# Bulk loads on another engine's DMA queue, the first keys split on another engine, and the first stacks loaded in halves, in a two-attention kernel on one core

## The chip, the cores and the metric

The kernel runs on one core of one Trainium2 chip. The metric is the time on the device of one execution, in microseconds (us), lower is better.

## The reference

The input x is 16 x 256 x 128 in float32 (16 batches, T = 256 rows, D = 128). Four blocks follow each other, each adding to x:

```
x = x + attention_a(layernorm(x))     # softmax, q and k rotated by position (rope), 16 heads of 8
x = x + ffn(layernorm(x))             # silu(x Wg) * (x Wu), then Wd; integer weights / 127, hidden 384
x = x + attention_b(layernorm(x))     # causal, sparsemax instead of softmax, 16 heads of 8
x = x + ffn(layernorm(x))
```

## The kernel before

**Items and steps.** The work is cut into 32 items: item n below 16 is the softmax attention and the feed-forward of batch n ("soft"), item n from 16 on the sparsemax attention and feed-forward of batch n - 16. All engines run one list of steps, `for step in range(FIRST_STEP, LAST_STEP)`, each doing what is its own in a step. An item has 16 heads and starts 16 steps behind the one before it. `AT`, `PLAIN` and `SECOND` say at which step (16 n + offset) each piece of item n is due; `SECOND` has the offsets of item 1. Engines meet at semaphores alone, and each engine executes its own list in order. Steps below 0 are the lead-in: they make the queries and keys of items 0 and 1. From step 0 on, step 16 n + h forms head h's scores of item n (`pass1`, line 1452, two products), whose row maxima VectorE takes (`reduce_head`, line 1093). From step 30 on, `pass2` forms the scores again, transposed and with the maxima subtracted (line 1476), ScalarE takes the exponential (`probs`, line 1288), and `pv` (line 1498) multiplies by the values.

**Queries and keys of an item.** TensorE transposes the normalised x (line 1354), ScalarE copies it (`take_xT`, line 1233), TensorE projects q, k and v (lines 1368, 1378). VectorE adds the rotation's two terms (`rope_cos`, `rope_sin`, lines 1080, 1086). GpSimd adds them and splits the float32 result into three bf16 parts (`split`, lines 928 to 938: add, cast, subtract, cast, subtract). SyncE stores the parts in device memory (`store_q`, lines 778 and 779, 192 and 128 KB; `store_k`, line 784, 192 KB) and loads them back, rearranged, as stacks (`load_q` and `load_k`, lines 792 and 809, three transfers of 192 KB each). `pass1` of an item waits at head 0 until all six transfers are there. Four sets of stacks (`STACKS`) take turns. SyncE issues every transfer of the kernel, in one order; `load_shift` (line 813) brings the row maxima into the stacks and sits behind `load_q` of a later item.

**Once only.** Weights, constants and the later x are loaded by SyncE at steps given in `ONCE` and `X_REST`: wb 449 KB, two pieces of constants of 256 and 384 KB, wf 576 KB; x of items 3 and 4 (256 KB), 5 to 7 (384 KB), 8 to 11 and 12 to 15 (512 KB each). `load_mask_rows` (line 801) makes eight transfers of 384 KB, one every 16 steps from step 57 on. VectorE casts the masks and the weights at steps 24 and 40.

**Spare products.** `spare` (line 1506) is a product of the identity with itself whose result nobody reads. 34 of them are issued at step -16, 60 at step -10, and four in each of the steps 0 to 28 that have no projection or transposition (22 such steps).

## Time and profile before

| | |
|---|---|
| median of 3 runs | 628.57 us |
| the three runs | 627.22, 628.57, 633.52 us |
| profiled execution: span from first to last instruction | 625.7 us |
| median less that span | 2.9 us |
| TensorE busy | 596.2 us (95%) |
| VectorE, ScalarE, GpSimd busy | 487.5, 427.1, 390.2 us |

The profile records one execution. Its own time is not listed apart from its span, so the table sets the span beside the median: the 2.9 us are what lies around the span and what this execution was faster or slower than the median.

### The profile page before, as it was taken

To read this page: it belongs to the slowest core of one execution; us is meant where nothing else is said; L and a number is where in the kernel's file an instruction comes from. 1 tells how busy PE (TensorE), PEld (TensorE's weight loads), DVE (VectorE), ACT (ScalarE), POOL (GpSimd) and SP (SyncE) were. 2 spreads that over 40 slices of the span, in tenths; PEclk is the share of its full clock that TensorE was granted. 3 is DMA by queue.
4 is the path that set the end of the run, shared out by engine and by line. 5 is a ranking of instruction groups with operands and counts; after the bars stand their busy time and mean duration, and the time that the engine had idled before them with its cause. 6 is when DMAs were issued, how large, how long until landed. Compare 5 with 4: busy or idle time off the path is not lost.

```text
span 625.7 us, 19158 instructions
## 1 busy us (share of the span) xinstructions
PE 596.2 (95%) x6716; PEld 465.1 (74%) x6716; DVE 487.5 (78%) x1421; ACT 427.1 (68%) x1057; POOL 390.2 (62%) x824
## 2 busy tenths in 40 slices
PE   5897999999999999999999999999999999999985
PEld 4775556777677777676778888788888888888664
DVE  2297788888888888888788887787888888888332
ACT  2013677777877777788878777676777777777762
POOL 5754456676776666767766766577666666653332
PEclk9997999999999999999999999999999999999996
DMA  3597467766566645554454533433544444440000
GB/s 98 131 260 170 118 155 178 174 150 153 152 143 157 144 121 119 149 143 134 123 141 124 133 95 97 119 104 84 123 111 121 111 116 106 114 120 20 13 10 21
DMA packets 73760, 75.91 MB, mean 121 GB/s; under 512 B 10236, under 2 KB 68156, under 8 KB 69052
## 3 DMA queue, kind: packets, MB, share of 16 engines
q1 hardware_dynamic: 73660, 74.64, 47.3%
q8 instruction: 55, 0.90, 0.6%
q14 instruction: 45, 0.37, 0.2%
HBM read 46.86 MB, written 23.33 MB: 112 GB/s over the span
## 4 chain that ended last, share of the span: by engine, by line
PE 73%; DMA 6%; DVE 5%; issue 5%; POOL 4%; ACT 3%; SPq 2%; POOLq 0%; ACTq 0%; DVEq 0%
PE banks L1498 15%; PE banks L1476 8%; PE banks L1452 8%; PE banks L1429 7%; PE banks L1368 5%; PE banks L1420 4%; PE banks L1421 3%; PE banks L1455 3%; PE banks L1461 2%; PE banks L1400 2%; PE banks L1485 2%; PE banks L1479 2%; DMA q_image<-qk_parts 2%; PE banks L1457 2%; PE banks L1459 2%
## 5 line engine op out<-in xcount | busy, mean ns | idle before, releaser
L1288 ACT ACTIVATE probs_t<-banks 128x512 f32<-128x512 f32 (+1 forms) x512 | 270.4, 550 | 82.5 <-PE banks L1476 53.8
L1093 DVE TENSOR_REDUCE neg_shift<-banks 128x2 f32<-128x512 f32 x256 | 166.3, 681 | 42.5 <-PE banks L1452 41.2
L1498 PE MATMUL banks<-probs_t,v_ext 128*32 128x256 f32 (+1 forms) x2048 | 117.8, 359 | 0.0
L1452 PE MATMUL banks<-k_stack,q_stack 72*128 72x256 bf16 x512 | 100.5, 278 | 6.7 <-DVE neg_shift L1093 2.5
L1099 DVE MAX8 top<-banks 128x8 f32<-128x256 f32 x256 | 106.1, 415 | 0.0
L1476 PE MATMUL banks<-q_stack,k_stack 75*128 75x256 bf16 x512 | 100.1, 277 | 1.0 <-DMA q_stack<-neg_shift_rows 0.9
L984 POOL TENSOR_TENSOR hidden<-up_tanh,gate_half 128x256 f32<-128x256 f32 x96 | 69.9, 731 | 48.1 <-DVE up_tanh L1139 42.2
L1098 DVE MAX8 top<-banks 128x8 f32<-128x128 f32 x256 | 74.5, 291 | 31.6 <-PE banks L1461 29.2
L1498 PEld LDWEIGHTS banks<-probs_t,v_ext 128*32 128x32 f32 x2048 | 55.5, 109 | 40.1 <-issue 13.3
L1452 PEld LDWEIGHTS banks<-k_stack,q_stack 72*128 72x128 bf16 x512 | 41.3, 98 | 45.8 <-DVE neg_shift L1093 32.8
L1420 PE MATMUL banks<-f_xT_high,w_gate_up 128*128 128x256 f32 x192 | 58.8, 328 | 0.9 <-DVE f_xT_low L1131 0.9
L1479 PE MATMUL banks<-q_stack,k_stack 123*128 123x128 bf16 x256 | 57.0, 223 | 2.8 <-ACT probs_t L1288 2.2
L1461 PE MATMUL banks<-mask_b,ident_b 128*128 128x160 bf16 x256 | 59.6, 233 | 0.0
L1485 PE MATMUL banks<-maskT_b,ident_b 128*128 128x160 bf16 x256 | 59.6, 233 | 0.0
L1455 PE MATMUL banks<-k_stack,q_stack 123*128 123x128 bf16 x256 | 56.6, 221 | 2.6 <-DVE top L1099 2.5
L1481 PE MATMUL banks<-q_stack,k_stack 75*128 75x128 bf16 x256 | 56.3, 220 | 0.0
L1457 PE MATMUL banks<-k_stack,q_stack 72*128 72x128 bf16 x256 | 56.2, 220 | 0.0
L1459 PE MATMUL banks<-k_stack,q_stack 123*128 123x128 bf16 x256 | 56.1, 219 | 0.0
L1483 PE MATMUL banks<-q_stack,k_stack 123*128 123x128 bf16 x256 | 56.1, 219 | 0.0
L916 POOL TENSOR_TENSOR f_rstd<-f_var_eps,neghalf 128x2 f32<-128x2 f32 x32 | 23.0, 720 | 50.3 <-DVE f_var_eps L1071 50.2
L928 POOL TENSOR_TENSOR qk<-rope_cos_terms,rope_sin_terms 128x256 f32<-128x256 f32 x32 | 23.2, 725 | 49.9 <-DVE rope_sin_terms L1086 49.8
L1476 PEld LDWEIGHTS banks<-q_stack,k_stack 75*128 75x128 bf16 x512 | 46.6, 99 | 10.2 <-issue 1.2
(108 smaller groups left out, 1389.4 us busy)
## 6 DMA issues: line engine op xcount, KB each, us to landing
q_stack<-q_image SPq DMA_DIRECT2D x96, 192.0 KB
k_stack<-k_image SPq DMA_DIRECT2D x96, 192.0 KB
q_image<-qk_parts SPq DMA_DIRECT2D x32, 192.0 KB, 2.3
k_image<-qk_parts SPq DMA_DIRECT2D x32, 192.0 KB, 2.1
q_image<-qk_parts SPq DMA_DIRECT2D x32, 128.0 KB, 2.2
o_image<-out_t SPq DMA_DIRECT2D x32, 128.0 KB, 1.9
out_compact<-o_image SPq DMA_DIRECT2D x32, 64.0 KB
rdenominators<-r_image SPq DMA_DIRECT2D x16, 128.0 KB, 2.3
```

The costliest lines, as they stand in the source:

```text
L984: pool.tensor_tensor(m.hid[:, c, :], m.t1[:, k, :], m.g05[:, k, :], ALU.mult).then_inc(hid_ready, 1)
L1093: dve.tensor_reduce(m.nm[:, n % STACKS, h, :], scores.rearrange("p (q k) -> p q k", q=TT), AX.X, ALU.max, negate=True).then_inc(reduced, 1)
L1098: dve.max(m.z8[:, n % 2, h, 0, :], scores[:, 0:P])
L1099: dve.max(m.z8[:, n % 2, h, 1, :], scores[:, P:P + T]).then_inc(reduced, 1)
L1288: act.activation(m.pt[:, (n * Q + g) % GROUPS, i, 0:size], shifted_banks[:, j % 2, 0:size], ACT.Exp if is_soft(n) else ACT.Relu, scale=SCA ...
L1420: pe.matmul(out, w[:, c * P:(c + 1) * P], m.f_high[:, :], start=True, stop=False)
L1452: ins = pe.matmul(scores[:, qt * T:(qt + 1) * T], qs[0:STACK, h, qt * P:(qt + 1) * P], ks[0:STACK, h, :], start=True, stop=True)
L1455: pe.matmul(scores[:, 0:P], qs[0:MASKED, h, 0:P], ks[0:MASKED, h, 0:P], start=True, stop=True, skip_group_check=True)
L1461: ins = pe.matmul(blocks(scores, REST), m.ident_b[:, :], twice(m.mask_b, REST), start=False, stop=True, skip_group_check=True)
L1476: ins = pe.matmul(shifted[:, kt * T:(kt + 1) * T], ks[0:SHIFTED, j, kt * P:(kt + 1) * P], qs[0:SHIFTED, j, :], start=True, stop=True)
L1485: ins = pe.matmul(blocks(shifted, REST), m.ident_b[:, :], twice(m.maskT_b, REST), start=False, stop=True, skip_group_check=True)
L1498: ins = pe.matmul(out_bank[32 * i:32 * i + 32, at + skip:at + T], v_windows(v, kt)[:, Q * g + i, :], m.pt[:, (n * Q + g) % GROUPS, i, kt * ...
```

## The change

Five edits:

1. The bulk loads (x from item 3 on, wb, two pieces of constants, wf) and the eight `load_mask_rows` are issued by ScalarE instead of SyncE. wb, the constants, wf and x of items 3 and 4 are due at step -22, which is behind ScalarE's copy of item 0 at step -23. Items 5 to 7 of x are due at step 1 (before at 11).
2. `split_k` of item 0 moves from GpSimd to VectorE, where it stands right behind item 0's `rope_sin` for the keys and ahead of item 1's statistics.
3. Item 0's stacks are loaded in two halves of heads, 12 transfers of 96 KB in place of six of 192 KB. The order on SyncE is: queries heads 0 to 7, queries heads 8 to 15, keys heads 0 to 7, keys heads 8 to 15. `pass1` of item 0 waits for the first halves at head 0 and for the second halves at head 8.
4. The four loads of ones into the key stacks (line 860) move from step -7 to step -31, ahead of all stores.
5. Spare products: 12 instead of 60 at step -10, three instead of four in the steps from 0 on; the 34 at step -16 stay.

```
-ONCE = dict(set_v=-14, ones=-7, wb=6, masks=8, wf=12, sum_bias=20, fold_bias=22, cast_masks=24, cast_weights=40)
-X_REST = {1: (3, 5), 11: (5, 8), 27: (8, 12), 43: (12, 16)}
-SPARE = {-16: 34, -10: 60}
-SPARE_SCORES = 4
+ONCE = dict(set_v=-14, ones=-31, bulk=-22, sum_bias=20, fold_bias=22, cast_masks=24, cast_weights=40)
+X_REST = {-22: (3, 5), 1: (5, 8), 27: (8, 12), 43: (12, 16)}
+SPARE = {-16: 34, -10: 12}
+SPARE_SCORES = 3
...
             def store_q(n):
                 sp.wait_ge(q_split, n + 1)
                 wait(sp, q_loaded, q_loads(n) * SEM)
+                if n == 1:
+                    sp.wait_ge(first_q_loaded, PARTS * SEM)
...
             def load_q(n):
...
+                first = H // 2 if n == 0 else 0
+                for rep in range(PARTS if n == 0 else 0):
+                    rows = slice(rep * PARTS * HD, (rep + 1) * PARTS * HD)
+                    sp.dma_start(m.qs[r][rows, 0:first, :], q_rows[rep * HD:(rep + PARTS) * HD, 0:first])\
+                      .then_inc(first_q_loaded, SEM)
                 for rep in range(PARTS):
                     rows = slice(rep * PARTS * HD, (rep + 1) * PARTS * HD)
-                    sp.dma_start(m.qs[r][rows, :, :], q_rows[rep * HD:(rep + PARTS) * HD]).then_inc(q_loaded, SEM)
+                    sp.dma_start(m.qs[r][rows, first:H, :], q_rows[rep * HD:(rep + PARTS) * HD, first:H])\
+                      .then_inc(q_loaded, SEM)
...
-                if (n := due(step, "split_k")) is not None:
+                if (n := due(step, "split_k")) is not None and n > 0:
                     split(n, 1)
...
+            def split_first_k():
+                qk = m.qk[:, 1, :]
+                high, middle, low = (m.parts[:, s, 1, :] for s in range(PARTS))
+                wait_freed(dve, "k", 0)
+                dve.tensor_tensor(qk, m.tc[:, 1, :], m.ts[:, 1, :], ALU.add).then_inc(k_step, 1)
+                dve.wait_ge(k_step, 1)
+                dve.tensor_copy(high, qk).then_inc(k_step, 1)
+                dve.wait_ge(k_step, 2)
+                dve.tensor_tensor(qk, qk, high, ALU.subtract).then_inc(k_step, 1)
+                dve.wait_ge(k_step, 3)
+                dve.tensor_copy(middle, qk).then_inc(k_step, 1)
+                dve.wait_ge(k_step, 4)
+                dve.tensor_tensor(low, qk, middle, ALU.subtract).then_inc(k_split, 1)
...
                     rope_sin(n, 1, "k")
+                    if n == 0:
+                        split_first_k()
...
+            def load_weights():
+                act.dma_start(m.wb[:, :], io["wb"]).then_inc(wb_loaded, SEM)
+                act.dma_start(m.cc[:, CC["invk"]:], io["consts"][:, CC["invk"]:CC_COLS]).then_inc(masks_loaded, SEM)
+                act.dma_start(m.co[:, :], io["consts"][:, CC_COLS:]).then_inc(masks_loaded, SEM)
+                act.dma_start(m.wf_int[:, :], io["wf"]).then_inc(wf_loaded, SEM)
+
             for step in range(FIRST_STEP, LAST_STEP):
+                if step in X_REST:
+                    first, end = X_REST[step]
+                    act.dma_start(m.x[:, first * TT:end * TT, :], x_d[:, first * TT:end * TT, :])\
+                       .then_inc(x_rest_loaded[x_piece(first)], SEM)
+                if step == ONCE["bulk"]:
+                    load_weights()
+                n, j = divmod(step - 3 * H, H)
+                if 0 <= n < 2 * STACKS and j == 9:
+                    load_mask_rows(*divmod(n, 2))
                 if (n := due(step, "take_out")) is not None:
                     take_out(n)
...
-                if h == 0:
+                if n == 0 and h == 0:
+                    pe.wait_ge(first_q_loaded, PARTS * SEM)
+                    pe.wait_ge(first_k_loaded, PARTS * SEM)
+                if h == (H // 2 if n == 0 else 0):
                     pe.wait_ge(q_loaded, q_loads(n + 1) * SEM)
                     pe.wait_ge(k_loaded, (n + 1) * (3 * SEM))
```

`store_k` and `load_k` are changed as `store_q` and `load_q`; `load_mask_rows` is the same function with `act` in place of `sp`.

## Rows read from the trace of the kernel before

**Rows 1.** Stages: length; PE, PEld, DVE, ACT, POOL busy (count); clock; DMA share; GB/s.

```profile
28.18:54.13 25.95, 23.30 (x180) 17.67 (x181) 24.53 (x54) 3.20 (x9) 11.44 (x26) 1.00 0.76 206
54.13:78.00 23.87, 21.91 (x170) 13.57 (x170) 16.89 (x35) 13.92 (x29) 11.28 (x24) 0.79 0.62 143
...
102.00:160.00 58.00, 57.89 (x561) 41.86 (x562) 50.68 (x119) 44.34 (x103) 40.75 (x83) 1.00 0.65 154
```

**Rows 2.** The chain, 13 to 29 us: start, length, what.

```profile
13.69 0.68 POOL a_rstd L908
...
17.99 2.08 DMA k_image<-qk_parts
...
20.83 7.22 DMA k_stack<-k_image
```

**Rows 3.** Timeline of the lead-in: start, length, engine, line, operation, [idle before].

```profile
11.67 0.47 DVE L1086 SCALAR_TENSOR_TENSOR rope_sin_terms<-banks,wa,cc 128x256 f32<-128x256 f32 x1
...
14.14 0.49 SPq L779 DMA_DIRECT2D q_image<-qk_parts  x1
...
18.39 1.26 SPq L792 DMA_DIRECT2D q_stack<-q_image  x3
...
19.40 6.71 PE L1506 MATMUL banks<-ident_b 128*128 128x256 bf16 x60
...
28.18 0.38 PE L1452 MATMUL banks<-k_stack,q_stack 72*128 72x256 bf16 x2 [2.07 <-DMA k_stack<-k_image]
...
28.60 2.67 DVE L1093 TENSOR_REDUCE neg_shift<-banks 128x2 f32<-128x512 f32 x4 [8.50 <-PE banks L1452]
```

**Rows 4.** Two stretches: length, TensorE busy, clock, DMA share, GB/s.

```profile
8.00:14.00 6.00, 6.00 (x26) 1.00 0.00 0
...
33.00:48.00 15.00, 14.09 (x113) 1.00 0.90 260
```

**Rows 5.** The chain of waits, 0 to 110 us: two pieces.

```profile
41.70 6.54 DMA q_image<-qk_parts
...
102.73 1.00 PE banks L1498 x16
```

**Rows 6.** Timeline 49 to 68 us: SyncE's queue and TensorE.

```profile
49.42 0.73 SPq L813 DMA_DIRECT2D q_stack<-neg_shift_rows  x1
...
52.01 0.39 PE L1452 MATMUL banks<-k_stack,q_stack 72*128 72x256 bf16 x2 [0.76 <-DVE neg_shift L1093]
...
54.13 0.41 PE L1476 MATMUL banks<-q_stack,k_stack 75*128 75x256 bf16 x2 [0.86 <-DMA q_stack<-neg_shift_rows]
...
57.59 0.59 PE L1452 MATMUL banks<-k_stack,q_stack 72*128 72x256 bf16 x2 [1.35 <-issue]
...
60.10 0.63 PE L1452 MATMUL banks<-k_stack,q_stack 72*128 72x256 bf16 x2
...
60.96 0.63 PE L1452 MATMUL banks<-k_stack,q_stack 72*128 72x256 bf16 x2
...
61.95 1.94 PE L1498 MATMUL banks<-probs_t,v_ext 128*32 128x256 f32 x16
```

**Rows 7.** Where the clock falls and returns: length, TensorE busy, clock, DMA.

```profile
54.25:54.50 0.25, 0.25 (x3) 0.70 0.65 131
...
64.50:64.75 0.25, 0.25 (x4) 0.82 0.00 0
```

**Rows 8.** Lines of VectorE: duration ns min/median/max, first and last start.

```profile
L1110 DVE SCALAR_TENSOR_TENSOR top_sums<-top_sums,cc x16: 424/604/718, 322.5 to 580.3; 128x256 f32<-128x256 f32 x16
L1151 DVE CAST maskT_b<-x x1: 219/219/219, 48.2 to 48.2; 128x128 bf16<-128x128 f32 x1
```

**Rows 9.** Steady state near 207 us, and line 801 over the run.

```profile
206.72 0.37 ACT L1233 COPY a_xT<-banks 128x256 f32<-128x256 f32 x1
...
207.47 1.03 PE L1368 MATMUL banks<-a_xT,wa 128*128 128x256 f32 x4
...
L801 SPq DMA_DIRECT2D q_stack<-mask_rows x4: 672/678/688, 101.9 to 208.2; - x4
```

34 lines of the change are left out of this document (14 added, 20 removed).

## The prediction

> **What bounds the kernel now.** I read the table of stages first. Behind 102 us TensorE is the bound: 57.89 of 58.00 us busy, and the chain of waits holds hardly anything else there. Nothing in the change takes work from that part, so it can only start sooner, or be slowed. What can be won lies ahead of it. Up to 28.18 us no head is scored; between 28.18 and 54.13 VectorE is busy 24.53 of 25.95 us and TensorE 23.30, partly with spare products; from 54.13 to 78 TensorE's mean granted clock is 0.79 [rows 1].
>
> The chain then says what the lead-in waits for. GpSimd is done with item 0's queries at 13.69 us and, behind item 1's small statistics, with its keys just ahead of 17.99; the store of the keys takes 2.08 us; the last load of a key stack is issued at 20.83 and lands 7.22 us later [rows 2]. SyncE had issued the store of the queries by 14.63, but stood at the store of the keys, so that the query stacks went out only at 18.39 [rows 3]. TensorE fills the wait with 60 spare products until 26.11, idles 2.07 us and scores at 28.18 [rows 3].
>
> The third view is the stretch from 33 to 48 us, where the bulk loads are issued: the DMA engines are 0.90 busy at 260 GB/s, while from 8 to 14 us they move nothing [rows 4]. A store of item 2's queries in that stretch takes 6.54 us [rows 5], against 2.08 for the store of item 0's keys [rows 2]. SyncE waits for it before it issues the shift rows at 49.42 and item 2's keys behind them; TensorE idles 0.86 us for the first and 1.35 us ahead of 57.59, where item 2 begins, for the second by my reading (the profile says "issue") [rows 6]. The clock falls near 54.4 us and is back near 64.6 [rows 7], after TensorE had idled 0.76 us for VectorE ahead of 52.01 and 0.86 us ahead of 54.13 [rows 6].
>
> **The change part by part.** The sum is made against the profiled execution: 625.7 us of span, and the 2.9 us to the median that no edit touches.
>
> *Keys of item 0 on VectorE.* `rope_sin` ends at 12.14 [rows 3]. Five instructions follow. The nearest row to a 128x256 operation with two inputs in SBUF is line 1110, 0.42 to 0.72 us, median 0.60; the nearest cast is 128x128 at 0.22, so 128x256 costs 0.22 to 0.44 [rows 8]. Three at 0.50, two at 0.35 and five hand-overs of about 0.07 (the gaps of GpSimd's chain) give 2.55 us: the keys are split at 14.7 (bounds 14.0 and 15.5) and not at 17.97 or so, and their store follows that of the queries. What is queued behind it on VectorE is item 1's statistics, 1.0 us of work, now done near 15.7; GpSimd's `rstd_a`, which started at 13.69 [rows 2], then starts 2 us later, and ScalarE's normalisation and TensorE's transposition of item 1 likewise. Item 1 is scored 16 steps behind item 0, more than 10 us later than its queries are stored, which covers that. GpSimd, rid of 3.1 us of split, gives the time back to item 1.
>
> Here a rule speaks against the edit. The 0.42 to 0.72 us of line 1110 for one shape [rows 8] show that such an operation sometimes takes longer. The Trainium skill, "SBUF — State Buffer", on the engine side of SBUF, says that an operation of VectorE with two SBUF inputs and one of GpSimd that reads SBUF take a port pair in turn, as an exclusive lock, the loser fully blocked. By that rule the two splits, side by side from 12.2 to 13.7, would be served one after the other and both be done near 15.5, which delays the query store by about 1.3 us and takes 1.0 us off the sum below (622.1 instead of 621.1); the trace has no such pair to show it.
>
> *Loads of item 0.* SyncE no longer stands at the keys. The query store lands 2.1 us behind 14.14, at 16.2 to 16.6 us, and the loads start there instead of at 18.39. Before, 1152 KB took from 18.39 to 28.05: 2.1 us of latency and 7.56 us of transfer. Head 0 now needs all of the queries and half of the keys, 864 KB, because the second halves of the queries stand ahead of the first halves of the keys: 5.67 us. That gives 16.6 + 2.1 + 5.7 = 24.4, and 24.5 for the first score. Six more issues of about 0.4 us each fit beside this transfer, since the ninth is out at 20.4. I add 0.6 us for what of the bulk is still moving and for items 5 to 7 of x, whose 384 KB ScalarE now issues near 22 us. First score at 25.1 instead of 28.18: 3.1 us (bounds 1.0 and 4.2). The second halves land some 2 us later and are needed eight steps, over 5 us, later.
>
> *Ones ahead.* Four issues of SyncE move to where it has nothing else; they leave its queue behind the key loads. Worth nothing in themselves.
>
> *Bulk loads at step -22.* ScalarE issues five transfers, 1.92 MB, between 7.2 and about 10.5 us, with nothing due on it until item 1. At 260 GB/s [rows 4] they take 7.4 us, until about 16. The DMA engines were idle for most of this. The two stalls go [rows 6]: 0.86 + 1.35 = 2.2 us (bounds 0.9 and 2.2). What is late next at step 30 is VectorE, at step 32 the keys of item 2, which should land 2 to 4 us before TensorE asks for them, although 512 KB of x (items 8 to 11) leaves ScalarE at about the same moment.
>
> *Clock.* If the second idle gap before 54.4 goes, I expect the clock to stay. At the low level two heads of item 2 are 0.86 us apart [rows 6], at the high level VectorE's pace is 0.67 [rows 3]; eight steps give 1.5 us. The sixteen products of line 1498 take 1.94 us there [rows 6], 1.00 at the high level [rows 5]. Together 2.4, of which I take 2.0, since VectorE and ScalarE are late next (bounds 0 and 3).
>
> *Fewer spares in the steps.* 22 steps lose 0.11 us of TensorE each, 2.4 us. But VectorE needs 0.63 to 0.67 per step, so most is not on the path; 0.8 us (bounds 0 and 2).
>
> *Mask rows on ScalarE.* Eight issues of 0.68 us each [rows 9] at a step where ScalarE next has to copy the transposed x, which it ends at 207.09; TensorE projects from it at 207.47 [rows 9]. The slack is 0.38, so a whole issue ahead of the copy costs 0.3 us, eight 2.4 us; with no slack at all 5.4; nothing if the queue issues while the preceding exponential still runs. No row here shows an issue on ScalarE. I take 0.6, near the lower end, because the copy is the only instruction near it with a reader close behind, and half of each issue fits into its slack. Moving them off SyncE gains nothing: TensorE does not wait for a transfer behind 102 us.
>
> *Fewer spares at step -10.* 48 products of 0.112 us [rows 3], 5.4 us less. With item 1's projections until about 21.3, the twelve end at 22.6, 2.5 us ahead of the first score. The work isn't on the path; the cover it gives the clock is the first rival.
>
> Sum: 3.1 + 2.2 + 2.0 + 0.8 - 0.6 = 7.5 us. 625.7 becomes 618.2, and 628.6 becomes 621.1 us.
>
> **The rivals.**
>
> (A) *The clock is low at the first scores and comes back.* Before, an idle gap of 2.07 us was survived; now it is 2.5 us or more, with another of over 1 us ahead of item 1's transposition, which comes 2 us later while the 34 spares ahead of it stay as they are. A step would cost two times 0.43 + three times 0.22, about 1.09 us, instead of 0.67; lasting about as long as the low stretch seen at most, 10 us [rows 7], and 6 us at least, it loses 0.39 of that time: 2.3 to 4.0 us. About 624.3. For: two scattered gaps sufficed before 54.4. Against: the 2.07 us did not.
>
> (B) *The low clock near 54 us stays.* TensorE waits for VectorE between steps 25 and 32 whether or not the transfers are in time, and the spares have become fewer. 2.0 us less won: 623.1; with the 1.35 us wait also still there, because of the x that ScalarE issues, 624.5.
>
> (C) *The bulk lies across the first stores.* The 1.92 MB move until 16 us, the query store leaves at 14; if it takes 6.54 us as item 2's did [rows 5], the loads start at 20.7, and the first score comes at 28.6 to 29. The 3.1 us are lost and half a microsecond more: 624.7. On what the queue as such brings, the Trainium skill, "DMA: Bandwidth & Descriptors", § Issuing engines are not separate DMA queues, says that transfers of all issuing engines run on the same 16 DMA engines and interleave, so that a second engine saves only issue time. By that rule the bulk costs the same transfer time wherever it is issued, and all of the gain must come from the time at which it is sent; the trace has one issuing queue and can't show it.
>
> (D) *Mask rows at full price*, 2.4 to 5.4 instead of 0.6: 622.9 to 625.9.
>
> (E) *Slower: the low clock stays through all scores without `pass2`.* The products of line 1452 have 72 rows; after 57.59 TensorE was busy without a gap and stayed low for 7 us, until behind the first products of line 1498. With three spares and not four, it might not come back before step 30. Then 22 steps cost 0.43 us more, 9.5, and the transpositions and projections of items 2 and 3 about 4.5 more, 14 in all: 621.1 + 14 = 635.1. It decides from the point where the clock is still low at step 8 or so; its condition is rival A and no return.
>
> That the change does not do what it says has no room: the order of issues is written out.
>
> **How the numbers follow.** The forecast has 0.42, A 0.15, B 0.18, C 0.10, D 0.08, E 0.07. The likeliest is 621.1. About 1% of the time, 6.3 us, is what a measurement of this kernel can tell from no change, so faster means below 622.3. The forecast lies 1.2 us beyond that; most of its own spread (616.5 to 623) is there, 0.38, and of B, A and D the better ends and mixtures that win more at the start, 0.10: faster 0.48. Slower by over 1% is E: 0.07. The rest, 0.45, is within 1%. The range goes down to 616.5, where the start gives 4.2, the clock 3, the steps 2 and the mask rows nothing, less some of it, and up to 627.5, which takes in A to D and pairs of them; outside it are E and a little on either side.
>
> **What would show it.** First products of line 1452 at 25.1 us; the key store right behind the query stores near 15; DMA busy and not idle from 8 to 14; no waits of TensorE for the shift rows at step 30 and for item 2's keys; granted clock 1.00 from the first score to the end phase, where A and E would show 0.50 behind 25 us, B near 50 to 60; ScalarE's copy of line 1233 in the steps of the mask rows no more than 0.3 us later than in other items. I am wrong if the query store takes more than 3 us, if a slice ahead of the last has a clock under 0.9, or if TensorE gets gaps near the mask rows.

## The result and the profile after

The changed kernel takes 625.78 us, the kernel before 629.57 (medians of 20 executions each); the ratio is 0.994 with a 95% interval of 0.991 to 0.997. So the change wins 3.8 us, where 7.5 were forecast.

Three numbers of each execution explain the difference: its time, its span, and its mean granted clock. Over 121 executions of the kernel before, taken in five batches with the experiments, time less span is 3.45 us; over the 20 of the changed kernel it is 1.78 (1.74 to 1.82, no overlap with the other's 2.67 to 3.72). One more execution of the kernel before took 823.13 us, at a mean clock of 0.658, and is left out of all means. So 1.7 us of the gain lie outside what the profile shows. Within a kernel the time falls as the clock rises: a straight line through the 121 executions falls 367 us per unit of mean clock, through the 20 455. I use 400, and call **span at full clock** the mean of span - 400 x (1 - clock). It is 620.1 before and 616.5 after: 3.6 us are won inside the span. The mean clock is 0.9844 (standard error 0.0005) before and 0.9804 (0.0014) after, and this gives 1.6 us back. 3.6 + 1.7 - 1.6 = 3.7. With 367 or 455 in place of 400, the 3.6 becomes 3.5 or 3.9. Without the executions that lie over 1.5% above the fastest of their kernel (8 of before, 3 of after), the gain inside the span is 3.8 us and the loss of clock 0.0030, worth 1.2.

How the part inside the span divides between 3.6 and -1.6 is an estimate: a mean clock doesn't say where the clock was low, and a microsecond at the low level costs nothing where TensorE would have waited anyway, as in the lead-in below. Inside the span, at whatever clock, the mean falls from 626.4 to 624.3, by 2.1 us.

The pair of profiles shows more than the change is worth, 6.4 us of span: the profiled execution of after is the fastest of its 20, 621.09 us with a span of 619.3. The stages after, in the columns of [rows 1], and the stretch that answers to [rows 4]:

```profile
24.00:50.00 26.00, 22.23 (x166) 15.55 (x165) 23.66 (x53) 3.20 (x9) 14.69 (x31) 1.00 0.65 164
50.00:74.00 24.00, 22.32 (x214) 13.61 (x216) 21.50 (x46) 17.25 (x37) 14.17 (x31) 1.00 0.61 159
98.00:156.00 58.00, 57.97 (x566) 41.74 (x565) 50.46 (x118) 44.76 (x104) 41.67 (x85) 1.00 0.62 150
8.00:14.00 6.00, 6.00 (x29) 4.96 (x28) 3.43 (x7) 0.00 (x0) 2.93 (x5) 1.00 1.04 259
```

From 8 to 14 us the DMA engines now move the bulk at 259 GB/s, where they moved nothing. The stage from 50 to 74 has the clock at 1.00, where [rows 1] show 0.79. The stage from 98 is what it was. From the first score on, the clock of this execution stays at 1.00 until the end phase, where it is low for 16 us with TensorE busy for little over half of the time:

```profile
603.00:619.00 16.00, 8.96 (x39) 7.42 (x37) 3.42 (x9) 3.23 (x9) 3.16 (x6) 0.50 0.07 20
```

So most of what brings its mean clock down to 0.984 lies in the end phase, which no edit touches.

The lead-in, in the columns of [rows 3]:

```profile
11.88 0.67 POOL L929 TENSOR_TENSOR qk<-qk,qk_parts 128x256 f32<-128x256 f32 x1
12.25 0.58 DVE L1088 TENSOR_TENSOR qk<-rope_cos_terms,rope_sin_terms 128x256 f32<-128x256 f32 x1
12.62 0.47 POOL L931 CAST qk_parts<-qk 128x256 bf16<-128x256 f32 x1
12.86 0.37 DVE L1090 CAST qk_parts<-qk 128x256 bf16<-128x256 f32 x1
13.17 0.67 POOL L933 TENSOR_TENSOR qk_parts<-qk,qk_parts 128x256 bf16<-128x256 f32 x1
13.27 0.85 DVE L1092 TENSOR_TENSOR qk<-qk,qk_parts 128x256 f32<-128x256 f32 x1
13.86 0.39 SPq L782 DMA_DIRECT2D q_image<-qk_parts  x1
14.15 0.29 DVE L1094 CAST qk_parts<-qk 128x256 bf16<-128x256 f32 x1
14.30 0.48 SPq L783 DMA_DIRECT2D q_image<-qk_parts  x1
14.48 0.43 DVE L1096 TENSOR_TENSOR qk_parts<-qk,qk_parts 128x256 bf16<-128x256 f32 x1
...
14.93 0.47 SPq L790 DMA_DIRECT2D k_image<-qk_parts  x1
...
17.38 1.16 SPq L799 DMA_DIRECT2D q_stack<-q_image  x3
18.10 0.44 PE L1387 MATMUL banks<-cc,a_xhat 128*128 128x128 f32 x2 [2.04 <-ACT a_xhat L1261]
...
21.02 1.18 SPq L818 DMA_DIRECT2D k_stack<-k_image  x3
...
24.27 0.38 PE L1488 MATMUL banks<-k_stack,q_stack 72*128 72x256 bf16 x2
```

The keys are split at 14.91, the loads of the stacks start at 17.38 instead of 18.39, and the first head is scored at 24.27 instead of 28.18, 3.9 us earlier. TensorE does not wait for it: its twelve spare products have just ended. The clock falls once on the way, behind the 2.04 us of idle ahead of item 1's transposition (length, then TensorE, weight loads, VectorE, ScalarE and GpSimd busy, clock, DMA share, GB/s):

```profile
19.00:19.25 0.25, 0.25 (x1) 0.25 (x2) 0.00 (x0) 0.25 (x2) 0.25 (x1) 1.00 0.63 180
22.50:22.75 0.25, 0.25 (x3) 0.25 (x3) 0.17 (x1) 0.00 (x0) 0.18 (x2) 0.50 0.62 164
22.75:23.00 0.25, 0.25 (x4) 0.24 (x4) 0.25 (x2) 0.00 (x0) 0.25 (x1) 0.95 0.74 180
```

The wait of [rows 6] for the shift rows is gone and that for item 2's keys is halved, to 0.69 us; two others stand beside it:

```profile
28.12 0.36 SPq L790 DMA_DIRECT2D k_image<-qk_parts  x1
...
30.18 1.10 SPq L818 DMA_DIRECT2D k_stack<-k_image  x3
...
37.60 0.38 PE L1488 MATMUL banks<-k_stack,q_stack 72*128 72x256 bf16 x2 [1.17 <-issue]
...
51.55 0.38 PE L1488 MATMUL banks<-k_stack,q_stack 72*128 72x256 bf16 x2 [0.69 <-issue]
...
73.74 0.74 ACTq L1332 DMA_DIRECT2D k_stack<-mask_rows  x1
74.19 0.81 SPq L822 DMA_DIRECT2D q_stack<-neg_shift_rows  x1
...
75.12 3.32 SPq L818 DMA_DIRECT2D k_stack<-k_image  x3
...
82.65 0.38 PE L1488 MATMUL banks<-k_stack,q_stack 72*128 72x256 bf16 x2 [1.27 <-issue]
```

They stand where items 1, 2 and 4 begin: 1.17 + 0.69 + 1.27 = 3.1 us, against the 2.2 of [rows 6]. These are waits of one execution each: e1 has the same instructions up to the mask rows, and its profile has 2.14 us for item 1's keys. The third is plain to read: 384 KB of mask rows leave ScalarE's queue at 73.74, and SyncE's three issues of item 4's keys take 3.32 us instead of the 1.1 at 30.18. On ScalarE itself no price of the mask rows is seen; the last of the eight stands for the others:

```profile
197.55 0.62 ACTq L1332 DMA_DIRECT2D q_stack<-mask_rows  x1
197.58 0.87 ACT L1261 ACTIVATE a_xhat<-x,a_norm_bias,a_rstd 128x128 f32<-128x128 f32 x2
...
199.01 0.37 ACT L1244 COPY a_xT<-banks 128x256 f32<-128x256 f32 x1
```

The issue and the activation behind it run side by side, at all eight.

### The profile page after: what moved, and what is told of

Its sections match the earlier page's. It is cut to its first block, busy times and chain, and to the rows that moved or that the text cites. A ratio compares the mean times of both kernels' runs of the same rounds, so it can differ in the third digit from the quotient of the medians.

```text
span 619.3 us, 19025 instructions
## 1 busy us (share of the span) xinstructions
PE 587.7 (95%) x6646; PEld 458.0 (74%) x6646; DVE 489.8 (79%) x1426; ACT 427.2 (69%) x1057; POOL 388.2 (63%) x819
## 4 chain that ended last, share of the span: by engine, by line
PE 79%; DVE 8%; issue 4%; ACT 3%; POOL 2%; DMA 2%; SPq 1%; POOLq 0%; ACTq 0%; DVEq 0%
PE banks L1534 16%; PE banks L1488 10%; PE banks L1512 9%; PE banks L1401 7%; PE banks L1462 7%; PE banks L1453 3%; PE banks L1454 3%; PE banks L1491 3%; DVE neg_shift L1102 3%; PE banks L1433 2%; PE banks L1497 2%; PE banks L1521 2%; PE banks L1515 2%; PE banks L1411 2%; PE banks L1493 2%
## 5 line engine op out<-in xcount | busy, mean ns | idle before, releaser
L1488 PE MATMUL banks<-k_stack,q_stack 72*128 72x256 bf16 x512 | 98.9, 274 | 7.2 <-DVE neg_shift L1102 3.3
L1512 PE MATMUL banks<-q_stack,k_stack 75*128 75x256 bf16 x512 | 98.4, 273 | 0.1
L1488 PEld LDWEIGHTS banks<-k_stack,q_stack 72*128 72x128 bf16 x512 | 39.9, 97 | 47.0 <-DVE neg_shift L1102 36.0
L1462 PE MATMUL banks<-wf,hidden 128*128 128x128 f32 x384 | 51.0, 285 | 3.5 <-POOL hidden L979 3.5
```

What stands on the lines that cost most here:

```text
L1462: ins = pe.matmul(bank("down", n)[:, tt * D:(tt + 1) * D], m.hid[:, c, tt * P:(tt + 1) * P], down_w[:, c * D:(c + 1) * D], start=(c == 0), ...
L1488: ins = pe.matmul(scores[:, qt * T:(qt + 1) * T], qs[0:STACK, h, qt * P:(qt + 1) * P], ks[0:STACK, h, :], start=True, stop=True)
L1512: ins = pe.matmul(shifted[:, kt * T:(kt + 1) * T], ks[0:SHIFTED, j, kt * P:(kt + 1) * P], qs[0:SHIFTED, j, :], start=True, stop=True)
```

## The experiments

Eighteen kernels ran, in five batches, each compared with the kernel before on the same chip. The last two batches (e13 to e15, e16 to e18) look for the cause of the time outside the span and of the longer spans that came with it.

| kernel | executions | median us | ratio, 95% | mean clock | outside the span | span at full clock |
|---|---|---|---|---|---|---|
| before | 121 | 629.6 | | 0.984 | 3.45 | 620.1 |
| after | 20 | 625.8 | 0.991 to 0.997 | 0.980 | 1.78 | 616.5 |
| e1 | 6 | 621.9 | 0.980 to 0.990 | 0.985 | 1.80 | 615.1 |
| e2 | 12 | 626.3 | 0.991 to 0.997 | 0.986 | 1.79 | 618.2 |
| e3 | 12 | 628.9 | 0.995 to 1.002 | 0.979 | 1.80 | 619.6 |
| e4 | 12 | 629.7 | 0.999 to 1.005 | 0.982 | 3.45 | 619.5 |
| e5 | 12 | 628.1 | 0.995 to 1.001 | 0.979 | 1.80 | 618.0 |
| e6 | 8 | 633.9 | 1.004 to 1.009 | 0.979 | 3.40 | 622.2 |
| e7 | 12 | 627.7 | 0.991 to 0.998 | 0.980 | 1.79 | 617.5 |
| e8 | 6 | 619.9 | 0.982 to 0.989 | 0.990 | 1.78 | 614.7 |
| e9 | 12 | 624.1 | 0.989 to 0.994 | 0.990 | 1.80 | 618.0 |
| e10 | 12 | 628.3 | 0.996 to 1.004 | 0.981 | 1.79 | 619.2 |
| e11 | 12 | 630.4 | 0.997 to 1.004 | 0.980 | 3.43 | 619.2 |
| e12 | 6 | 621.1 | 0.980 to 0.991 | 0.986 | 1.78 | 613.9 |
| e13 | 8 | 630.8 | 0.998 to 1.004 | 0.986 | 1.81 | 623.4 |
| e14 | 7 | 633.4 | 1.001 to 1.008 | 0.980 | 3.69 | 621.5 |
| e15 | 8 | 629.8 | 0.998 to 1.007 | 0.978 | 1.79 | 620.2 |
| e16 | 10 | 630.5 | 0.996 to 1.004 | 0.978 | 1.80 | 619.6 |
| e17 | 4 | 624.3 | 0.981 to 0.997 | 0.990 | 1.74 | 618.0 |
| e18 | 10 | 630.2 | 0.998 to 1.003 | 0.984 | 1.80 | 621.6 |

The standard error of the last column is 0.1 in its first row, up to 0.8 in that of e1 and 0.3 to 0.6 in the others; that of a mean clock is 0.001 to 0.003. The ratio is to the kernel before in the same batch.

**e1: the mask rows back on SyncE.** In the changed kernel, `load_mask_rows` and its call move back:

```
-                act.dma_start(stack[SHIFTED:MASKED, :, :], src).then_inc(mask_rows_loaded, SEM)
+                sp.dma_start(stack[SHIFTED:MASKED, :, :], src).then_inc(mask_rows_loaded, SEM)
```

> The changed kernel, with the eight loads of mask rows back on SyncE's queue, in their old place behind the key stacks. Theory W (waits: the gain is given back at transfers that are now late): the first of these loads, sent by ScalarE at 73.7 us, runs beside item 4's key stacks, whose three issues take 3.3 us instead of 1.3, and TensorE waits 1.27 us ahead of 82.65; behind SyncE's own queue it comes after the key stacks, so this wait goes, and the queries of items 6 to 15 are projected 1.0 to 1.4 us earlier than in the changed kernel; median 1.2 us lower. Theory C (clock: fewer spare products let the granted clock fall more often, and that takes back the gain): nothing changes, within 0.5 us. A third view, that the issues themselves hold up ScalarE, would give over 2 us; the trace of the changed kernel shows none of it.

Measured 621.9, with the span at full clock 1.4 us under the changed kernel's, with an error of 0.9. The wait ahead of item 4, 1.27 us, is gone: sent by SyncE, the mask rows stand behind the keys again. A wait for transfers where item 4 begins, 1.27 to 3.06 us, stands in the profiles of all ten kernels with the mask rows on ScalarE (after, e2, e3, e6, e7, e10, e11, e15, e16, e17) and in none of the ten with them on SyncE. So the effect on this wait is shown. That the wait is the 1.4 us is likely and not shown: in e1's profile item 1's wait is 0.97 us longer, which takes most of it back.

**e2: spare products restored in part.** In the changed kernel:

```
-SPARE = {-16: 34, -10: 12}
-SPARE_SCORES = 3
+SPARE = {-16: 50, -10: 12}
+SPARE_SCORES = 4
```

> The changed kernel with more spare products: 50 instead of 34 at step -16, which fill the idle time of 2.04 us ahead of item 1's transposition, and four instead of three in the steps from 0 on; the twelve at step -10 stay. Theory C: the low clock of 19 to 22.6 us goes, the granted clock is low less often over the executions (mean 0.985 or more instead of 0.980), and the median comes down by 2 to 4 us. Theory W: the clock's mean is as before the edit, and four spares make the steps at most 0.8 us longer in all: median the same to 1 us higher.

The median stays at 626.3. The clock rises from 0.980 to 0.986, worth 2.3 us, and the span at full clock grows by 1.7: the gain in clock is taken back in time. Where that time goes isn't shown: the first score comes at 24.37 (24.27 in the changed kernel), and the fourth product of the steps costs nothing between e1 and e8 (615.1 and 614.7, with an error of 0.9). With 50 spares the clock holds in the lead-in, and now TensorE waits for the loads:

```profile
24.37 0.38 PE L1488 MATMUL banks<-k_stack,q_stack 72*128 72x256 bf16 x2 [1.50 <-DMA k_stack<-k_image]
```

So the loads are there near 24.3 us; a low stretch of 3.4 us as in the changed kernel is hidden behind them. The low clock is not only a matter of the lead-in. Where item 9 begins TensorE waits 1.55 us, and then (columns of [rows 1]):

```profile
158.62 0.38 PE L1488 MATMUL banks<-k_stack,q_stack 72*128 72x256 bf16 x2 [1.55 <-issue]
```

```profile
159.00:168.00 9.00, 9.00 (x66) 5.72 (x65) 5.21 (x13) 5.01 (x13) 6.02 (x14) 0.62 0.69 179
168.00:177.00 9.00, 9.00 (x89) 6.49 (x88) 7.66 (x19) 6.59 (x16) 3.53 (x7) 1.00 0.54 123
```

66 products in nine microseconds instead of 89, with TensorE busy all the time.

**e3: item 1's split ahead of the value fill.** In the changed kernel the fills of `v_ext` on GpSimd move from step -14 to -11, ahead of which item 1's keys are then split:

```
-ONCE = dict(set_v=-14, ones=-31, ...
+ONCE = dict(set_v=-11, ones=-31, ...
```

> The changed kernel with GpSimd's filling of the value tiles of items 1 to 3 moved from step -14 to step -11, behind the splits of item 1's queries and keys. Theory W: item 1's keys are late (split at 28.1, loaded at 30.2, TensorE idle 1.17 us at step 16, ahead of 37.60); now they are split near 24.5, the wait of 1.2 us goes, and the queries of item 3 and later come 1 us earlier unless another wait takes it; median 0.5 to 1.2 us lower. Theory C: no change, 0.5 us either way. Against both: item 1's stores and loads now follow so close behind item 0's second halves that those may come late for head 8, which would show as an idle gap of TensorE near 30 us.

It lost 3.1 us at full clock and at the median. Item 1's wait went, as expected. But the fills now stood ahead of item 2's small statistics: `a_rstd` ran at 32.64 us, and TensorE stood for it ahead of 34.81:

```profile
34.81 0.69 PE L1387 MATMUL banks<-cc,a_xhat 128*128 128x128 f32 x2 [2.97 <-ACT a_xhat L1261]
```

The new wait is larger than the 1.17 us that the edit was to remove. The profiled execution took 637.26 us, 8 us above the median, so the sizes of its waits are its own; the order of the instructions is not. Moving an instruction has two ends, also in an experiment.

**e4: fewer spares alone.** The kernel before with edit 5 only:

```
-SPARE = {-16: 34, -10: 60}
-SPARE_SCORES = 4
+SPARE = {-16: 34, -10: 12}
+SPARE_SCORES = 3
```

> The kernel before with only the fifth edit: 12 instead of 60 spare products at step -10, three instead of four in the steps from 0 on. Theory C: an idle gap of 7 us ahead of the first scores lowers the clock at 28 us in nearly every execution, and the time is 2 to 4 us above the kernel before. Theory W: the clock matters little here; VectorE sets the pace of the steps from 0 on, so the time is that of before, within 1 us, or up to 0.8 us less.

The median is 629.7, as before: 0.6 us less at full clock, 0.002 less clock, worth 0.9. TensorE stood 7.06 us ahead of its first score, at 27.72, and the first scores ran at the low clock, two steps in 2.08 us (1.17 in e7, at the high clock):

```profile
27.72 0.58 PE L1452 MATMUL banks<-k_stack,q_stack 72*128 72x256 bf16 x2 [7.06 <-DMA k_stack<-k_image]
...
28.73 0.63 PE L1452 MATMUL banks<-k_stack,q_stack 72*128 72x256 bf16 x2
...
29.80 0.63 PE L1452 MATMUL banks<-k_stack,q_stack 72*128 72x256 bf16 x2
```

This is what rival A describes, in a kernel without the earlier start. A step with three spares takes 1.04 us here.

**e5: bulk loads back.** The changed kernel with edit 1 undone: bulk and mask rows on SyncE at their old steps.

```
-ONCE = dict(set_v=-14, ones=-31, bulk=-22, ...
-X_REST = {-22: (3, 5), 1: (5, 8), ...
+ONCE = dict(set_v=-14, ones=-7, wb=6, masks=8, wf=12, ...
+X_REST = {1: (3, 5), 11: (5, 8), ...
```

> The changed kernel with all bulk loads, mask rows and loads of ones back on SyncE at their old steps; the key split on VectorE, the halves and the fewer spares stay. Theory W: the first score stays near 24.3 us, but the waits of 0.86 us for the shift rows and of 1.35 us for item 2's keys are back, and item 4's wait of 1.27 us goes; 1 to 2 us slower than the changed kernel at the same granted clock. Theory C: no difference in the clock. Open besides: the time outside the span from first to last instruction is 3.4 us in the kernel before and 1.8 in the changed one; if ScalarE's use of its own queue is behind it, 3.4 us come back here and the total is 3 to 4 us slower.

1.5 us slower at full clock, 2.3 at the median. The waits of before are back, longer:

```profile
51.52 0.38 PE L1511 MATMUL banks<-q_stack,k_stack 75*128 75x256 bf16 x2 [1.03 <-DMA q_stack<-neg_shift_rows]
...
56.06 0.58 PE L1487 MATMUL banks<-k_stack,q_stack 72*128 72x256 bf16 x2 [3.28 <-issue]
```

In this kernel these waits are the bulk's. In e9 the bulk loads lie at the same steps and the first score 3.9 us later; the store of item 2's queries then leaves at 42.97 and is done within 3.5 us (6.54 in [rows 5]), the wait for the shift rows is absent and item 2's is 0.51. So the waits hang on where that store falls against the bulk, and not on the bulk's place alone. The first score is at 25.60, later than in the changed kernel though the loads are sent earlier, at 16.50. Here the clock stayed low for 6.8 us from 18 on, and TensorE was itself the last to be ready:

```profile
23.72 2.04 PE L1541 MATMUL banks<-ident_b 128*128 128x256 bf16 x12
25.60 0.38 PE L1487 MATMUL banks<-k_stack,q_stack 72*128 72x256 bf16 x2
```

**e6: item 0's keys on GpSimd again.** The changed kernel with edit 2 undone:

```
-                if (n := due(step, "split_k")) is not None and n > 0:
+                if (n := due(step, "split_k")) is not None:
```

> The changed kernel with item 0's keys split on GpSimd again. The key store leaves near 18.1 instead of 14.9 us, SyncE stands there and the query loads leave at 18.4 instead of 17.4; 6 + 3 issues follow, so the first score comes near 25.5 to 26.5 instead of 24.3; item 1's transposition is 1.5 us earlier, so its keys are in time for step 16 and that wait of 1.17 us is smaller. Theory W: 0.5 to 1.5 us slower than the changed kernel at the same clock, because part of the later start is a wait less. If the port pair shared by VectorE and GpSimd mattered, the query store would leave 0.1 to 0.3 us earlier. Theory C: clock as in the changed kernel or 0.002 higher, for the idle gap of 2.04 us ahead of item 1's transposition goes.

8.1 us slower than the changed kernel and 4 slower than the kernel before: without its keys in time, the rest of the change is a loss. The first score comes at 28.42:

```profile
18.62 1.27 SPq L799 DMA_DIRECT2D q_stack<-q_image  x3
...
19.58 0.40 ACTq L1341 DMA_DIRECT2D x<-x_in  x1
...
28.42 0.59 PE L1486 MATMUL banks<-k_stack,q_stack 72*128 72x256 bf16 x2 [7.71 <-DMA k_stack<-k_image]
```

I read this as a collision: ScalarE sends x of items 5 to 7 at 19.58, among the loads of the stacks. e11 tries it. The second issue of the query store is at 14.38, not 0.1 to 0.3 us earlier than the 14.30 of the changed kernel, as I had expected for a port that matters.

**e7: whole stacks.** The changed kernel with edit 3 undone, six transfers of 192 KB.

```
-                first = H // 2 if n == 0 else 0
+                first = 0
```

> The changed kernel with item 0's stacks loaded whole again, six transfers of 192 KB. The first score waits for 288 KB more: 1.5 to 2 us later, near 26.2 instead of 24.3, and six issues of 0.4 us less stand on SyncE. Theory W: half of it is covered by item 1's wait at step 16, so 0.8 to 1.5 us slower than the changed kernel at the same clock. Theory C: an idle gap ahead of the first score of 2 us where the changed kernel has none; clock 0.002 lower and 1 us more on top.

The first score is at 26.63, behind 1.02 us of idle: the halves bring the start forward by 2.4 us. At full clock 1.0 us of it remains in the end (error 0.6), 1.9 at the median. The rest is given back at once: TensorE waits only 0.48 us for item 1's keys here, 1.17 in the changed kernel: item 1's keys hardly depend on item 0's start.

**e8: e1 with four spares per step.** e1's edit and

```
-SPARE_SCORES = 3
+SPARE_SCORES = 4
```

> Mask rows on SyncE as in e1 and four spare products per step from step 0 on, the 34 and 12 of the lead-in as in the changed kernel. Theory C: with 88 instead of 66 products in the steps the clock's mean rises from 0.980 towards that of before, 0.986, worth 2 us, at a price of 0.8 us for the longer steps: a median of 622 to 623.5. Theory W: mask rows alone bring 1.2 us and the fourth product only costs: median near 624.5 to 625.5, clock's mean 0.980 to 0.983.

619.9, the best of all: 9.7 us under the kernel before and 5.9 under the changed one. Its clock is among the highest, 0.990. Up to 94 us TensorE stands for item 1's keys (1.42 us) and item 2's (1.19), and no more for item 4's. It has six executions; its interval ends at 0.989 and that of the changed kernel begins at 0.991. The median is below what either theory gave.

**e9: edit 2 alone.** The kernel before with `split_first_k` on VectorE.

```
+                    if n == 0:
+                        split_first_k()
```

> The kernel before with only the second edit: item 0's keys split on VectorE. The runs so far have 3.4 us outside the span in the three kernels that split these keys on GpSimd and 1.8 in all that do it on VectorE. Theory O (outside: this edit takes 1.6 us off the time outside the span, whatever else is changed): 1.8 us here. If it is another edit or a pair of them: 3.4. Inside the span: the query loads leave near 17 instead of 18.4 us, so the first score comes 1 to 1.5 us earlier, 27 instead of 28.2, and the spare products that end at 26.1 or later don't delay it. In all 2 to 3 us faster than the kernel before by theory O, 0.5 to 1.5 without it.

624.1: one edit of five gives no less at the median than all. At full clock the five edits are 1.5 us ahead of it (616.5 against 618.0, error 0.5), but they have a mean clock lower by 0.009, and that takes more away. Yet nothing starts earlier. The stacks are sent at 16.43, but the first score is at 29.45:

```profile
22.90 6.71 PE L1522 MATMUL banks<-ident_b 128*128 128x256 bf16 x60
...
29.45 0.38 PE L1468 MATMUL banks<-k_stack,q_stack 72*128 72x256 bf16 x2
```

The 60 spares, which were cover before, are the bound here: the edit puts back item 1's transposition and projections, at 18.07 instead of 16.28 and at the low clock, and the spares behind them begin at 22.90 instead of 19.40. I had expected that they delay nothing. The gain is 1.7 us outside the span, 2.1 at full clock inside it (items 1 and 2 have more time for their keys, and TensorE stands for a transfer only 0.51 us), and 0.005 of clock, worth 2.

**e10: five more instructions on GpSimd.** The changed kernel with five single-column fills, which makes GpSimd's number of instructions that of before (824):

```
+    m.pad = sb("pad", [P, 8])
...
+                if step in (20, 21, 22, 23, 24):
+                    pool.memset(m.pad[:, step - 20:step - 19], 0.0)
```

> The changed kernel with five small memsets on GpSimd, at steps 20 to 24, into a tile that nobody reads; GpSimd then has as many instructions as in the kernel before. If the time outside the span follows the length of GpSimd's program, it is 3.4 us here and the median 1.6 us higher than the changed kernel's. If it follows what VectorE or the order of the first splits does, it stays at 1.8 and nothing changes within 0.5 us at the same clock.

1.79 us outside the span: it is not GpSimd's number. But the span grew by 2.7 us at full clock, which five fills of 0.1 us don't explain.

**e11: e6 with the x later.** e6 and x of items 5 to 7 at step 20:

```
-X_REST = {-22: (3, 5), 1: (5, 8), 27: (8, 12), 43: (12, 16)}
+X_REST = {-22: (3, 5), 20: (5, 8), 27: (8, 12), 43: (12, 16)}
```

> e6 (item 0's keys on GpSimd, the rest changed) with the 384 KB of x for items 5 to 7 sent at step 20 instead of step 1. In e6 ScalarE sent them at 19.6 us, beside the key stacks, TensorE idled 7.7 us ahead of the first score at 28.4, and the total was 8 us above the changed kernel. Theory X (the collision with this one load is what delays the first score): the first score comes near 26, the clock doesn't fall ahead of it as deep, and the total is 3 to 6 us below e6. Rival: the key stacks are late because their store is, and the load costs nothing: first score at 28 or later, total within 1.5 us of e6.

First score at 25.41, 3.0 us earlier than e6's, and 3.0 us less at full clock (error 0.7), 3.5 at the median: the collision is shown.

**e12: e8 with the x later.** e8 and the line of e11.

> e8 (mask rows on SyncE, four spare products per step) with the same load of x at step 20, near 36 us, when the DMA engines are idle before item 2's stores. Theory W: item 1's key stacks, for which TensorE waits 1.2 to 2.1 us at step 16, are loaded between 29 and 37 us, behind this load's place in e8 (23 to 26.5), so the wait stays; 0 to 0.5 us faster than e8. If its traffic held back the second halves and with them item 1's stores: the wait shrinks by 1 us and the median comes to 619. It should be the fastest of all kernels or equal to e8; against the changed kernel 3 to 5 us faster.

621.1, at full clock 0.8 us under e8, which is within the errors. Item 1's wait goes, and item 2's grows to 2.43 us. The sum of the two hardly changes, 2.6 and 2.4. Why item 2's grows isn't shown: the 384 KB leave at 36.80, beside its query store, but its keys leave at 43.89, 1.0 us earlier than in e8, and in both the 512 KB of x for items 8 to 11 follow them by 0.5 us.

**e13, e14, e15: more instructions on VectorE.** The fills of e10 on VectorE: five in the kernel before (e13), one there (e14), five in the changed kernel (e15).

```
+                if step in (20, 21, 22, 23, 24):
+                    dve.memset(m.pad[:, step - 20:step - 19], 0.0)
```

> The kernel before, with five single-column fills on VectorE in steps 20 to 24; nothing else. If what lies outside the span hangs on the number of VectorE's instructions (1421 before, 1426 after and here), it is 1.8 us here and not 3.4. If it hangs on the split's place as such, it stays at 3.4. The span is 625 to 627 either way: the fills cost VectorE some 0.1 us each.

> The kernel before with one such fill on VectorE. By the number theory this is between: 3.4 or 1.8 us outside the span, and either tells where the edge lies. By the other theory 3.4.

> The changed kernel with five such fills on VectorE (1431 instructions). 1.8 us outside the span if the number matters only up to an edge, or if it doesn't matter; 3.4 would say that it goes to and fro with the number.

Outside the span 1.81 us in e13, 3.69 in e14, 1.79 in e15. With 1421 or 1422 instructions VectorE goes with 3.4 to 3.7 us, with 1426 or 1431 with 1.8, whether or not any work has moved. So the 1.7 us outside the span come with edit 2's five more instructions on VectorE and have nothing to do with the keys. No run tried a number between 1422 and 1426, or said what happens outside the span. The spans of all three are longer, by 3.3, 1.4 and 3.7 us at full clock; a single fill of 0.1 us can't do that. What they share with e10 is the tile `pad`: 32 bytes of each partition, which moves all tiles behind it, the stacks among them, from addresses that are multiples of 64 to ones that are not.

**e16, e17, e18: the tile.** e16 is the changed kernel with the 32-byte tile and no fill. e17 and e18 are e15 and e13 with a tile of 64 bytes:

```
+    m.pad = sb("pad", [P, 16])
```

> The changed kernel with the unused 32-byte tile ahead of the stacks and no padding instruction: the stacks lie 32 bytes further and no longer at multiples of 64. If the address costs the time, it is 2 to 4 us over the changed kernel at the same clock (about 628), with 1.8 us outside the span. If the fills cost it, it equals the changed kernel (625.8).

> The changed kernel with five fills on VectorE and a tile of 64 bytes, so that the stacks stay at multiples of 64. By the address theory it equals the changed kernel (625.8; e15, with 32 bytes, took 629.8). By the other it is as e15.

> The kernel before with the five fills and a tile of 64 bytes. By both theories of this batch together: span as before, 1.8 us outside the span in place of 3.4, so about 628, 1.6 us below the kernel before, without anything of the change. If the fills cost time in the span, about 631 as e13.

e16 is 3.1 us slower at full clock than the changed kernel, with no instruction added. Its transfers take longer; the rows are issue, queue, count, KB each and median us from issue to landing, first of the changed kernel:

```profile
x<-x_in ACTq DMA_DIRECT2D x2, 512.0 KB, 6.2
...
x<-wf_in ACTq DMA_DIRECT2D x1, 576.0 KB, 7.6
...
x<-x_in ACTq DMA_DIRECT2D x1, 384.0 KB, 3.3
```

and of e16:

```profile
x<-x_in ACTq DMA_DIRECT2D x2, 512.0 KB, 7.9
...
x<-wf_in ACTq DMA_DIRECT2D x1, 576.0 KB, 8.4
...
x<-x_in ACTq DMA_DIRECT2D x1, 384.0 KB, 4.3
```

These are one execution each. The targets of these three lie ahead of the moved tiles; that they are slow because the transfers beside them are is my reading, no run separates it. TensorE then waits at the items' beginnings:

```profile
53.91 0.58 PE L1489 MATMUL banks<-k_stack,q_stack 72*128 72x256 bf16 x2 [2.94 <-issue]
...
89.83 0.38 PE L1489 MATMUL banks<-k_stack,q_stack 72*128 72x256 bf16 x2 [3.06 <-issue]
```

With 64 bytes and five fills of 0.06 us the price is 1.5 us at full clock in either kernel (e17 618.0 against 616.5, error 0.6, with four executions; e18 621.6 against 620.1, error 0.4); with 32 it was 3.3, 1.4 and 3.7 with fills on VectorE and 2.7 in e10. The fills by themselves cost nothing that the errors show (e15 less e16 0.6, error 0.9), but no run has the tile of 64 bytes without them. So my expectation for e17 and e18, no price at all, was wrong, and the rule "multiples of 64" is not the whole of it. The first stack lies at byte 73216 of its partition in the kernel before and in the changed one, and every stack at a multiple of 256; both the 32 and the 64 bytes take them off it. A boundary of 128 or 256 bytes would fit all these runs; none tries a tile of 128 or 256 bytes. Settled is that a tile of 32 bytes that nobody uses costs this kernel 3.1 us (error 0.7); by which boundary, and for which tile, is open. The number of instructions holds again: 1.74 and 1.80 us outside the span.

## Why the prediction came out as it did

The sum was 3.1 + 2.2 + 2.0 + 0.8 - 0.6 = 7.5, measured 3.8, of which 1.7 lie outside the span: inside it, where all terms of the sum belong, 2.1. The time lies within the range; the size of the forecast does not hold. Two steps failed: the clock, put at +2.0 and measured near -1.6, and the waits, put at +2.2 and near -0.9 in the profiles. Term by term:

- **Start, 3.1: right, somewhat low.** 24.27 against a forecast of 25.1, 3.9 us. The key split ended at 14.91 (forecast 14.7). The loads started 0.8 us later than forecast (17.38) and were done near 24.3 all the same. The later start is the bulk's, in part: with the bulk elsewhere the loads leave 2.2 us behind the second issue of the query store (e5 and e9), here 3.1, and 2.5 in e1. e7 and e9 show how the parts hang together: the halves give 2.4 us of it; with all 60 spares the earlier keys give nothing. "The work isn't on the path" was true only of the kernel before; edit 5 is what lets edit 2 act.
- **The two stalls go, 2.2: one step that failed.** The wait for the shift rows went and that for item 2's keys fell from 1.35 to 0.69 us (e5 brings both back), but item 1's and item 4's came, and 3.1 us stand where 2.2 stood: the net is -0.9. The text named "what is late next" as VectorE at step 30 and item 2's keys in time by 2 to 4 us, and said of item 1 that "more than 10 us later ... covers that", counting from the store of its queries. Its keys come last: stored at 28.12, loaded from 30.18, and step 16 asks for them at 36.4. Before they were stored at 28.27, loaded from 32.41, and asked for at 40.44 without a wait. A start that comes 3.9 us earlier moves the need forward by 4.0; the store of the keys moves by 0.15 only, since item 1's transposition starts at 18.10 instead of 16.28 and GpSimd, though rid of item 0's keys, begins item 1's split at 21.83 instead of 21.99; the loads move by 2.2. The sum has no line for this slack. And the mask rows were priced on ScalarE's list of instructions only. Their price lies on the DMA engines: sent by another queue, they no longer wait behind item 4's keys (before, the keys left at 84.28 and the mask rows at 86.04) but share the engines with them. e1 gives 1.4 us for it, with an error of 0.9. The wait for item 2's keys, 0.69 us, fits what rival B said of it: they leave at 44.31, and 512 KB of x leave ScalarE at 44.82. No run separates it. All these waits are read from one execution of each kernel; the -0.9 can be off by 1 us.
- **Clock, 2.0: the step that failed most.** I read a stretch of 10 us in one execution and took it for the kernel's. The mean clock of before over 121 executions is 0.984, that of after is 0.980 over 20: 1.2 to 1.6 us are lost by the estimate above, not 2.0 won. The low clock moves from execution to execution: e8's profile has none near 54 us, e12's has 10.2 us there with an easier queue. On average more spares go with more clock: e2 lies 0.006 above the changed kernel (error 0.002), e8 0.006 above e1 (error 0.004). But they are not all of it: e9 has the spares of before and 0.990 against 0.984. So the cause of the 0.004 between before and after is open. e4 (0.982) points to the spares, with an error of 0.002. A rival is the lead-in: in all 12 profiles of kernels that split the first keys on VectorE and have the 34 spares at step -16, the clock is low for 3.4 or 6.8 us between 17.5 and 25, which is 0.003 or 0.006 of the mean, and in the profile of before it isn't; but e9 is one of them.
- **Fewer spares in the steps, 0.8:** e4 gives 0.6 at full clock (error 0.3) for both places together, and takes it back in clock. The fourth product alone costs nothing between e1 and e8.
- **Mask rows on ScalarE, -0.6:** nothing is seen as a price on ScalarE, since the issue runs beside its activations; the loss is on the DMA engines, as above.
- **Outside the span:** the text said that no edit touches it. Edit 2 took 1.7 us off it, and e13 gets the same from five fills that do no work. This is luck: without it the change would have won some 2 us.

In the span, at full clock: 3.9 - 0.9 + 0.6 = 3.6, as measured; that it fits to the tenth is luck, with an error of 0.4 on the 3.6, 0.3 on the 0.6 and about 1 on the -0.9.

**The rivals.** A (low clock at the first scores): the idle time came as it said, 2.04 us ahead of item 1's transposition, and the clock fell there, but it was back at 23.0, ahead of the first score, and its 3.4 us were hidden behind the loads. In the profiles of e3, e5, e7 and e15 it lasted 6.8 us, and in the three with halves the first score came at 25.3 to 25.7: the mechanism of A, at half of its smaller price (1.1 to 1.4 us against 2.3). The working of A has a slip: two times 0.43 + three times 0.22 is 1.52 and not 1.09; with 0.43 for the two products together it is 1.09, and e4 shows 1.04 for such a step. B (a wait ahead of item 2 stays) happened with 0.69 us. C (the bulk across the first stores) happened on a small scale: the loads leave 3.1 us behind the second issue of the query store (2.5 in e1), against 2.2 without the bulk, and not 6.54; the start came early all the same. But its mechanism, a transfer of another queue across a store or load that is waited for, is what happened at item 4 and in e6. D and E did not happen. All three signs of being wrong came: the store of the queries took over 3 us (3.1, up to the loads that wait for it), a slice near 20 us has a clock under 0.9 (the 3.4 us above), and TensorE gets a gap near the first mask rows.

**The two rules.** The first three steps of VectorE's split ran beside GpSimd's: its operations with two inputs took 0.58 and 0.85 us, and the last, alone, 0.43; GpSimd's cast beside it took 0.47 instead of 0.40. So there is a price: 0.65 us on VectorE, its cast included, and GpSimd's split of the queries takes 3.23 us from its first start to its last end instead of 3.15. The Trainium skill, "SBUF — State Buffer", § SBUF: two separate sides, calls this an exclusive lock with the loser fully blocked. The trace agrees: both of VectorE's two-input operations end 0.28 us behind the end of the GpSimd operation that had started before them (12.83 behind 12.55, 14.12 behind 13.84), and so they do, within 0.01 us, in the profiles of all 13 kernels with this split, also where the first started earlier and took 0.69 to 0.75 us (e3, e7, e15). What was wrong is the 1.3 us that I worked out from it: it counted whole splits, but only these operations wait, for what is left of the one in their way, and the keys were done at 14.91, not at 15.5. For the other, queues of different engines interleave on the same DMA engines (the Trainium skill, "DMA: Bandwidth & Descriptors", § Issuing engines are not separate DMA queues), the trace agrees at 75.12 us: three issues take 3.32 us beside 384 KB of another queue, and the keys come late. I had quoted it for the gain and did not turn it on the mask rows, where it told the loss.

## What to carry to other kernels

A transfer that moves to another queue loses its place behind the urgent ones: price it on the DMA engines, by what will be in flight beside it, and not only on its issuing engine. A start that is moved forward moves all needs behind it forward, so look up for each the slack it has then, from the last transfer it needs, and which filler work becomes the bound. Take a clock term from the mean over many executions and not from one profile, and before a difference of 1.5 to 3 us is put down to an edit, check that it hasn't changed a tile's address or the number of an engine's instructions.

## What the runs showed of the hardware that was not expected

- The mean time outside the span is 3.4 to 3.7 us with 1421 or 1422 instructions on VectorE and 1.7 to 1.8 with 1426 or 1431, in all 20 kernels; GpSimd's number (819 or 824) doesn't matter. Why, and where between 1422 and 1426 it changes, is open.
- An unused tile of 32 bytes ahead of the stacks costs 3.1 us (e16), one of 64 bytes together with five fills 1.5 (e17, e18). The stacks lay at multiples of 256 bytes without it. Which boundary counts is open.
- VectorE's operations with two inputs in SBUF end 0.28 us behind the GpSimd operation that was running when they started, in 26 of 26 cases.
- The low clock comes also in the middle of the run: behind a wait of 1.55 us the mean clock is 0.62 over 9.00 us in which TensorE is busy throughout (e2, 159 us).
- An issue of a transfer by ScalarE, 0.37 to 0.74 us, runs beside its activations.
- Three issues of SyncE for an item's keys take 3.32, 2.71, 3.56, 3.00 and 2.62 us at five of the eight items where 384 KB of another queue are in flight; in the kernel before, with one queue, most take 1.1 to 1.3, and the slowest 2.11.
